# The projection slabs are loaded from the GpSimd queue instead of the Sync queue

## What is computed

```python
xn = layernorm(x)
q = xn @ Wq.T;  k = xn @ Wk.T;  v = xn @ Wv.T
mem = cumsum(fft(k) * fft(v), axis=tokens)
attn = ifft(mem * conj(fft(q))).real
h = silu((xn @ w1.T) * s1) * ((xn @ w2.T) * s2)      # 1024 -> 4096
h = gelu((h @ h1.T) * sh1)                           # 4096 -> 4096
h = gelu((h @ h2.T) * sh2)                           # 4096 -> 4096
out = x + attn + (h @ w3.T) * s3                     # 4096 -> 1024
```

## Time and profile before

| What | us |
|---|---|
| runs shown, median of 2 | 8010.46 |
| lowest and highest of them | 7710.11 and 8310.82 |
| profiled execution | 7479.8 |
| its span on the slowest core, core 1 | 7478.3 |
| spans of the eight cores | 7456.6 to 7478.3 |
| TensorE (matmul) busy | 6147.5, 82% |
| GpSimd busy | 88.6, 1% |

### The profile page before, as it was taken

The page is one execution under the profiler, slowest core; times in us unless marked ns, Lnnn a source line. Parts: engine busy times, 40 slices in busy tenths (PEclk is TensorE's granted clock), DMA queues, the critical chain, the costliest instruction groups (busy, mean ns, idle before and its releaser), DMA issues.

```text
span 7478.3 us, 74368 instructions; the slowest of 8 cores (7456.6 to 7478.3 us)
## 1 busy us (share of the span) xinstructions
PE 6147.5 (82%) x31008; PEld 3041.8 (41%) x31008; DVE 937.4 (13%) x1519; ACT 521.4 (7%) x881; POOL 88.6 (1%) x160
## 2 busy tenths in 40 slices
PE   2878888840000899999999999999999999999999
PEld 1336566640000344444444444444444444444444
DVE  2112323210000210000021000012000001100000
ACT  2111111100000000000000000000000000000000
POOL 0000000000000000000000000000000000000000
PEclk6989899875555999999999999999999999999999
DMA  4114344369999233333423333332333332233333
GB/s 130 55 61 133 110 122 133 95 107 114 114 112 115 78 74 73 76 77 77 109 69 71 76 74 79 76 99 73 74 79 74 78 89 88 73 75 78 75 75 89
DMA packets 614490, 659.20 MB, mean 88 GB/s; under 512 B 14352, under 2 KB 587792, under 8 KB 611344
## 3 DMA queue, kind: packets, MB, share of 16 engines
q1 hardware_dynamic: 602704, 536.99, 29.1%
q0 software_dynamic: 11456, 117.45, 11.8%
HBM read 708.91 MB, written 130.02 MB: 112 GB/s over the span
## 4 chain that ended last, share of the span: by engine, by line
PE 78%; another core or an unknown queue 11%; DMA 5%; DVE 3%; issue 1%; ACT 1%; SPq 0%; DVEq 0%; ACTq 0%; POOLq 0%
PE ps L663 48%; PE ps L625 11%; PE ps L694 6%; PE ps L466 5%; PE ps L425 5%; PE ps L560 3%; DMA SLW<-w1b 2%; PE ps L326 1%; DMA SLA<-wl_v 1%; DMA SLB<-h1b 0%; DVE WLb L414 0%; DMA SLA<-wl_q 0%; DMA SLA<-wl_k 0%; ACT WHb L412 0%
## 5 line engine op out<-in xcount | busy, mean ns | idle before, releaser
L625 PE MATMUL ps<-XNFH,SLW 128*128 128x512 bf16 x2048 | 501.1, 389 | 910.3 <-issue 767.3
L663 PE MATMUL ps<-GH,SLB 128*128 128x512 bf16 x4096 | 913.0, 381 | 19.3 <-DMA SLB<-h1b 19.3
L663 PE MATMUL ps<-H1H,SLB 128*128 128x512 bf16 x4096 | 911.7, 381 | 11.0 <-DVE H1L L675 11.0
L663 PE MATMUL ps<-GL,SLB 128*128 128x512 bf16 x4096 | 904.9, 379 | 0.0
L663 PE MATMUL ps<-H1L,SLB 128*128 128x512 bf16 x4096 | 904.9, 379 | 0.0
L625 PEld LDWEIGHTS ps<-XNFH,SLW 128*128 128x128 bf16 x2048 | 200.3, 99 | 1171.9 <-issue 949.1
L663 PEld LDWEIGHTS ps<-GH,SLB 128*128 128x128 bf16 x4096 | 402.3, 98 | 509.8 <-issue 31.9
L663 PEld LDWEIGHTS ps<-H1H,SLB 128*128 128x128 bf16 x4096 | 402.0, 98 | 500.4 <-issue 21.9
L663 PEld LDWEIGHTS ps<-H1L,SLB 128*128 128x128 bf16 x4096 | 401.0, 98 | 483.1
L663 PEld LDWEIGHTS ps<-GL,SLB 128*128 128x128 bf16 x4096 | 400.9, 98 | 483.1
L625 PE MATMUL ps<-XNFL,SLW 128*128 128x512 bf16 x2048 | 488.2, 382 | 0.0
(11 more groups left out here) (103 smaller groups left out, 2625.9 us busy)
## 6 DMA issues: line engine op xcount, KB each, us to landing
SLA<-wl_k SPq DMA_DIRECT2D x64, 512.0 KB, 5.0
SLA<-wl_v SPq DMA_DIRECT2D x64, 512.0 KB, 4.7
SLA<-wl_q SPq DMA_DIRECT2D x64, 512.0 KB, 4.8
h1b<-h1c POOLq DMA_DIRECT2D x16, 2048.0 KB, 230.1
SLW<-w1b SPq DMA_DIRECT2D x32, 1024.0 KB, 5.4
SLW<-w2b SPq DMA_DIRECT2D x32, 1024.0 KB, 5.4
h2b<-h2c POOLq DMA_DIRECT2D x16, 2048.0 KB, 232.9
XT<-x_ds SPq DMA_DIRECT2D x8, 1024.0 KB, 8.3
```

Source lines behind the costliest of these rows:

```text
L625: ins = h.matmul(bank[:, 0:TF], sl[:, kc2, ol * 128:(ol + 1) * 128], lb[:, kc2, :], start=first, stop=(lb is XL and kc2 == KC - 1))
L663: ins = h.matmul(bank[:, 0:TF], sl[:, kc2, :], lb[:, kc2, :], start=first, stop=(lb is inL and kc2 == HC - 1))
```

## The change

One word. The load of a slab is issued by GpSimd instead of Sync. Source, destination, buffers, size and the order of the program's other operations stay as they are. The load now takes its place in GpSimd's queue, between the stores of lines 369, 372 and 579.

```diff
         def proj(wname, dstplane):
             for rc in range(KC):
                 sl = SLA[rc % 3]
-                S.op("sync", lambda h, s=wl_scr[wname], rc=rc, d=sl: h.dma_start(
+                S.op("gpsimd", lambda h, s=wl_scr[wname], rc=rc, d=sl: h.dma_start(
                     out=d[:],
                     in_=s[:, rc // 4, :, (rc % 4) * 256:(rc % 4) * 256 + 256]
                         .rearrange("c p (l m) -> p c l m", l=2)),
```

## The result

The changed kernel is slower: 7635 to 7654 us against 7479 to 7492 of the kernel before, ratio 1.0218, 95% interval 1.0205 to 1.0231. These figures, and all that follow, leave out executions in which one or both dies ran at a lower clock; the two runs that gave the 8010 were of that kind. The profiled execution's slowest core, core 2, has a span of 7636.4 us against 7478.3, 158 us more. I had forecast +136 us, 1.8%, and had the larger part of the chance on less than 2%. The direction and the mechanism held; one term was too small, and it lifted the result over the 2%.

What follows compares the result with a forecast made beforehand. TensorE bounds the attention stage, its slab loads nearly hidden. Tile seams 97, v 17, stalls 26, q -5 and first load 1 sum to 136 us: 7480 + 136 = 7616 us, +1.8%; forecast's own range 7575 to 7630, 7560 to 7750 with A and B.

Steps and rivals of the forecast that it cites:

- idle at 7 seams between tiles: Before k's slab 0 of the next tile: TensorE idle 12.0 us a seam, 6.4 late issue plus 5.6 load.
- slow start behind them: After each tile seam's idle time TensorE starts at the lower clock, adding 1.8 us.
- v's first slabs, late and slow: Seam from k to v: slab 0 3.6 us late instead of 2.0, plus 0.5 slow start; 17 us over eight tiles.
- stalls inside k and v (predicted with q's slab 7): Inside projections: 1.0 us stall at each third slab, five a tile, +3.3 a tile over existing stalls, 26 us.
- q, with its shorter wait for VectorE: q's slabs 0 to 3 start 1.6 us later under cover; the shorter wait and slow start give -5 us.
- first load of all: Very first slab load of the attention stage: +1 us.
- what stands ahead of a load: At tile seams k's loads queue behind XNH/XNL and eight part_scr stores; first issue at 1498.3, 6.4 us late.
- nothing is won back: Behind the attention stage: stores, casts and feed-forward follow as before, only later, so the 136 us stay.
- A: Rival: GpSimd's loads land clearly later than its stores, from 5.5 us on over 2% longer; at 6.2, 7670 us; chance 0.34.
- B: Rival: VectorE, busy 13.9 us, holds up GpSimd's loads of q: 134 us more, 7750; chance 0.04.
- C: Rival: faster, as Sync's first feed-forward loads get ahead of the casts, winning back more than 136 us; chance 0.04.
- D: Rival: the tile seam costs nothing, the stores finishing before TensorE; 39 us remain, 7519; chance 0.04.

Runs made afterwards that it cites:

- The kernel with 24 loads: Kernel before, with only k's slabs 0, 1 and 2 loaded from GpSimd, the other loads on Sync: 1.0139 of before.
- the pair with four buffers: Four slab buffers instead of three: in the kernel before (Sync) 7507 us beside 7487 to 7501; in the changed kernel (GpSimd) 1.0132 of before.
- unchained: Changed kernel, with the part_scr stores no longer waiting for each other's landing: 1.0148 of before.

## Why the prediction was right or wrong

The terms of the sum against the eight cores' timelines, changed less before, in us:

| term | predicted | measured |
|---|---|---|
| idle at 7 seams between tiles | 84 | 104 |
| slow start behind them | 13 | 15 |
| v's first slabs, late and slow | 17 | 14 |
| stalls inside k and v (predicted with q's slab 7) | 26 | 20 |
| q, with its shorter wait for VectorE | -5 | -1 |
| first load of all | 1 | 5 |
| sum | 136 | 157 |

**The step that failed** is the one on what stands ahead of a load: "the first load can be issued at its end, 1498.3, 6.4 us late". Measured are 8.9 us at seams 1 to 6 and 8.0 at the last. Two things were missing.

The first is a transfer that I had priced at nothing. I had written that `XT` is loaded earlier, and had asked only whether TensorE waits for it. It waits for its buffer, which VectorE's eighth addition frees. That addition waits for the landing of the sixth store, as the seventh store does, and so `XT` is issued 0.2 us behind the seventh store. I had taken the late eighth store of before (6.05 us) for the work of slab loads that would go, and put 2.61 in its place; but another transfer moved into the gap, and the pitch became 3.9. Without it the pitch is 2.8. That is shown by two kernels that hold `XT` back, by the one that leaves it where it was, and by the last seam of the changed kernel, which has none. This is 1.1 us a seam, 7 us in all. TensorE's idle time at these six seams fell by more when `XT` was held, from 14.9 to 12.8 us, 13 us in all; but at the last seam, where neither kernel loads `XT`, it differs as well, 13.6 against 12.6. So 1 us a seam between two kernels is scatter, and `XT`'s share is 7 to 13 us.

The second is that the pitch was read from one seam, the cleanest. From the second store to the seventh the seams of the changed kernel take 14.2 us on the mean where tile 6 of core 1 had 13.05, and in the kernel before the mean was already 14.5. This is about 1.1 us a seam, 8 us. With `XT` held it is 13.7, so a part of it may be `XT`'s. The load itself took 6.0 us from issue to start at the six seams, 5.6 in the sum, which is another 2 us. Together this is most of the 20 us that the first row of the table is short by. What disturbs single stores by 1 or 2 us, I haven't found out; no run tried it.

**What held.** The landing of GpSimd's loads, which no row of before showed: 5.2 us taken, 5.2 measured, from its 512 KB stores. The reaction, 0.60 taken, 0.58 measured. The difference in the first byte that the Trainium skill gives (DMA: Bandwidth & Descriptors, Specifications), 0.4 us, would have been too little alone: measured are 0.46 us of later reaction and 0.4 of later landing. The forecast that nothing is won back: what is behind the stage takes 5868 us against 5870. The waits for slabs: 192 us forecast, 190 measured on core 2. The kernel with 24 loads, 1.0139, and the pair with four buffers show the seam as the main part and reaction plus landing as the smaller, in the sizes of the sum.

**v and the slow starts.** v's slab 0 comes 1.0 us later on the mean, not 1.6. From the release of its buffer to its start it takes 6.0 us, 4.8 before: 1.2 more instead of 1.6, and 0.2 of this pass while slab 7 of k waits as well. Slab 1 of v waits 0.4 us less than before. But the slow start behind slab 0's pause, 2.9 us now and 1.9 before, became longer by 1.1 us on the mean (the slab takes 4.1 us instead of 3.0), not by 0.5; the counts below show how much oftener the longer pause has one. These errors nearly cancel. The first load of all is the row with the largest error for its size: TensorE starts 9.1 us behind its issue instead of 6.2. Why, was not tried.

**The rivals.** A (a landing of 5.5 us and more) did not come, though its result, over 2%, did. B is refuted: q's loads are issued in 882 to 893 ns while VectorE is busy, those of k in 882 to 907 without, and q did not grow. This agrees with the Trainium skill (SBUF — State Buffer, SBUF: two separate sides), by which only the copy of line 514 would count. C: Sync's loads did not overtake the casts. Its first of the feed-forward is issued at 1766.94 on core 2, behind the first cast at 1764.2, and lands in 256 us as before. D: the stores don't finish in time. Even unchained they end 1.8 us behind TensorE, and the load itself is still waited for. The chances were wrong in their split, not in the mechanism: with 136 forecast and 150 as the bound, each error of 2 us a seam decides, and the sum had no term for the disturbance of the stores.

## What to carry to other kernels

Before a load is moved to another queue, write down what will stand ahead of it there at the place where the loop turns: an eager load that becomes the last of a chain of stores, each awaiting the one before, costs the part of the chain that outlasts the engine waiting for it (8.9 us here) plus its own whole latency, and hoisting a few of them only moves the wait to the next. Then ask what the old queue will issue sooner now, and which transfer on the critical path it will meet. And take a pitch from all its repetitions, not from the cleanest one, above all when a bound is near.

## What the runs showed of the hardware

- A 512 KB load issued by GpSimd lands in 5.2 us (median), from Sync in 4.8. GpSimd's DMA begins 0.58 us after its wait is released, Sync's 0.12; each of these loads occupies GpSimd for 0.88 us, Sync for 0.36.
- The same load is 1024 packets of 512 bytes from Sync and 128 packets of 4096 bytes from GpSimd. For 192 loads the trace has 196608 packets of 512 bytes less and 24576 of 4096 bytes more.
- 1 MB of `XT` beside a 128 KB store makes that store's successor 1.1 us later (pitch 3.9 against 2.8), 2.0 us in the kernel with four buffers (4.8 against 2.7), and beside a 512 KB load it makes that load's start 2.5 us later (7.9 against 5.4) or 1.6 (7.1 against 5.5).
- In the changed kernel, all cores: after pauses of over 10 us TensorE's first slab took 4.0 to 5.3 us instead of 2.8 in 64 of 64 cases, after 3.5 to 10 us in 8 of 9, after 2.5 to 3.5 us in 80 of 101, after 1.5 to 2.5 us in 11 of 51, after 0.5 to 1.5 us in none of 269.
- Sixteen casts of 19 us of all DMA engines, put where no slab is needed, cost the attention stage nothing (1024 against 1025 us).
